# Where layer 2's weights, chunk 1's input blocks and tile 2's gathers stand in the start of a three-layer cross network

## The reference

```
inputs = emb[ids] * vals[:, :, None]            # 1024 x 39 x 16
h = inputs
for i in range(3):                              # 200 outputs each
    x = einsum('bhd,bmd->bhmd', h, inputs).reshape(B, -1, 16)
    x = relu(einsum('bcd,oc->bod', x, W[i]) + b[i][None, :, None])
    h, direct = (x[:, :100], x[:, 100:]) if i < 2 else (None, x)
    finals.append(direct)
cin = sum(concatenate(finals, 1), -1)
d = relu(relu(inputs.reshape(B, -1) @ D0.T + d0) @ D1.T + d1)
out = concatenate((cin, d), 1) @ fc_W.T + fc_b + sum(bias_emb[ids] * vals)
```

## Time and profile before

| | |
|---|---|
| median of 3 runs | 2751.63 us |
| profiled execution, its own time | 2752.34 us |
| its span | 2750.5 us |
| busy PE, DVE, ACT, POOL | 2649.5, 2285.0, 1834.6, 2249.6 us |
| chain that ended last, PE's share | 94% |
| PE idle before its first instruction | 62.6 us |

### The profile page before, as it was taken

How to read it: one execution, slowest core, us unless ns; L and a number is a source line. 1 busy time by engine, 2 the same in 40 slices (tenths; PEclk the granted TensorE clock), 3 DMA queues, 4 the chain that set the end, 5 groups by cost and what they waited for, 6 DMA issues and landing times.

```text
span 2750.5 us, 66670 instructions
## 1 busy us (share of the span) xinstructions
PE 2649.5 (96%) x17928; PEld 2640.2 (96%) x17928; DVE 2285.0 (83%) x4584; ACT 1834.6 (67%) x4776; POOL 2249.6 (82%) x1912
## 2 busy tenths in 40 slices
PE   0699999999999999999999999999999999999999
PEld 0599999999999999999999999999999999999998
DVE  2788888888888888888888888888888888888884
ACT  0576776766767667676777767677677766766663
POOL 6788888888888888888888888888888888877763
PEclk9799999999999999999999999999999999999999
DMA  8844545445444454544545455454554545545441
GB/s 149 199 124 123 133 126 130 124 118 144 116 133 125 118 149 112 136 121 122 146 111 138 120 131 137 114 136 118 138 131 118 133 117 140 129 117 136 111 115 51
DMA packets 199914, 349.82 MB, mean 127 GB/s; under 512 B 66632, under 2 KB 118697, under 8 KB 199615
## 3 DMA queue, kind: packets, MB, share of 16 engines
q1 hardware_dynamic: 185782, 342.81, 45.6%
q0 software_dynamic: 10496, 2.88, 3.1%
q10 hardware_dynamic: 3464, 2.68, 0.3%
HBM read 344.29 MB, written 14.17 MB: 130 GB/s over the span
## 4 chain that ended last, share of the span: by engine, by line
PE 94%; POOL 2%; SPq 2%; DVE 1%; issue 1%; DMA 1%; ACT 0%; POOLq 0%; ACTq 0%; DVEq 0%
PE acc L642 61%; PE acc L643 28%; PE acc L667 2%; POOL raw L498 1%; PE hrep L678 1%; DVE W L1061 0%; SPq L319 0%; DMA odd<-lin 0%; PE acc L742 0%; PE acc L743 0%; PE acc L744 0%; SPq L309 0%; DMA raw<-table,idx 0%; PE hrep L764 0%; PE hrep L766 0%
## 5 line engine op out<-in xcount | busy, mean ns | idle before, releaser
L642 PE MATMUL acc<-W,xhi_d 128*128 128x400 f32 x5632 | 1732.4, 367 | 17.2 <-DVE xlo_d L1087 10.6
L643 PE MATMUL acc<-W,xlo_d 128*128 128x200 f32 x5632 | 1434.9, 255 | 0.0
L1087 DVE TENSOR_TENSOR xlo_d<-prod_d,xhi_d 128x512 fp32r<-128x512 f32 (+1 forms) x1536 | 983.9, 641 | 205.1 <-ACT xhi_d L819 147.2
L1079 DVE TENSOR_TENSOR prod_d<-hrep,xrep 128x512 f32<-128x512 f32 (+1 forms) x1536 | 1039.0, 677 | 105.8 <-issue 27.7
L548 POOL TENSOR_TENSOR xlo_p<-prod_p,xhi_p 128x512 fp32r<-128x512 f32 (+1 forms) x768 | 953.8, 1242 | 181.3 <-ACT xhi_p L813 135.6
L642 PEld LDWEIGHTS acc<-W,xhi_d 128*128 128x128 f32 x5632 | 1059.9, 188 | 20.1 <-DVE xlo_d L1087 12.9
L643 PEld LDWEIGHTS acc<-W,xlo_d 128*128 128x128 f32 x5632 | 1078.4, 191 | 0.0
L819 ACT ACTIVATE xhi_d<-prod_d 128x512 fp32r<-128x512 f32 (+1 forms) x1536 | 885.1, 577 | 222.6 <-PE acc L643 199.8
L642 PE MATMUL acc<-W,xhi_p 128*128 128x400 f32 x2944 | 917.2, 363 | 12.9 <-POOL xlo_p L548 12.9
L542 POOL TENSOR_TENSOR prod_p<-hrep_s,xrep 128x512 f32<-128x512 f32 x512 | 665.9, 1301 | 161.3 <-ACT hrep_s L856 108.5
L643 PE MATMUL acc<-W,xlo_p 128*128 128x200 f32 x2944 | 751.7, 255 | 0.0
(11 more groups left out here) (92 smaller groups left out, 927.1 us busy)
## 6 DMA issues: line engine op xcount, KB each, us to landing
xrep<-xs SPq DMA_DIRECT2D x384, 384.0 KB
l0x<-xs SPq DMA_DIRECT2D x378, 136.5 KB
xrep<-xs SPq DMA_DIRECT2D x384, 128.0 KB
xrep<-xs SPq DMA_DIRECT2D x128, 336.0 KB
xrep<-xs SPq DMA_DIRECT2D x128, 64.0 KB
l0x<-xs SPq DMA_DIRECT2D x378, 19.5 KB
lin<-w SPq DMA_DIRECT2D x8, 750.0 KB
raw<-table,idx POOLq DMA_INDIRECT x328
```

Source lines behind the costliest of these rows:

```text
L642: pe.matmul(bank[:, 0:2 * OUTS], hi, w, start=first, stop=last, skip_group_check=True)
L643: return pe.matmul(bank[:, 0:OUTS], lo, w[:, 0:OUTS], start=False, stop=last, skip_group_check=True)
L1079: nc.vector.tensor_tensor(to, h, xrep[:, (par + layer - 1) % 2, a:a + count, :], ALU.mult).then_inc(s_prod_d, 1)
L1087: op = nc.vector.tensor_tensor(xlo_d[:, slot, 0:split], bank[:, 0:split], xhi_d[:, slot, 0:split].bitcast(F32), ALU.subtract)
```

## The change

Layer 2's rows are copied to DRAM by ACT's DMA queue, after layer 1's weights have landed and been rounded: three quarters ahead of ACT's first rounding of products, the last one behind it. ACT rounds all of layer 1's weights at that point. SP loads layer 2's weights before chunk 1's blocks. The five pieces of layer 2's weights are split in groups D0 to D4 of step 1 instead of D4 to D8, and the low part of piece 1 is made by POOL instead of DVE, in the middle of step 1. POOL gathers nothing in steps -1 and 0 and at the head of step 1: 4 rows at the end of step 1, 4 in each of steps 2 to 9 and 3 in step 10; its first pass through the loop is written out. For all tiles scaling, turning and storing come one step of the tile later.

```diff
-        W2_AT = {4: 0, 5: 1, 6: 2, 7: 3, 8: 4}
+        W2_AT = {0: 0, 1: 1, 2: 2, 3: 3, 4: 4}
-        def rows_of_weights(engine, layer, src):
+        def rows_of_weights(engine, layer, src, quarters):
...
@@ sync
-            rows_of_weights(sp, 2, w2)
-            sp.wait_ge(s_pt, 4)
             sp.wait_ge(s_prod_p, p_num(0, 1) + 1)
             load_layer0(2)
+            load_weights(sp, 2, w2)
+            sp.wait_ge(s_pt, 4)
             for e in (1, 2, 0, 3):
                 sp.wait_ge(s_xblk[e], BLOCK_SEM[e])
                 load_block(1, 1, e)
-            load_weights(sp, 2, w2)
...
-                    if j == 10:
+                    if j == 11:
                         store_inputs(k + 1)
-                    if j == 11:
+                    if j == 12:
                         store_dense_inputs(k + 1)
@@ gpsimd
-            FREE_AT = 8
+            FREE_AT = 9
             COUNTS = [2] * 5 + [3] * 9 + [2]
-            BEFORE = sum(COUNTS[0:DIM - 1 - FREE_AT])
+            FIRST = [4 * n + 4 for n in range(FREE_AT)] + [FIELDS]
...
+            product(1, 1, 2)
+            low(1, 1)
+            a, b = PIECES[2][1]
+            pool.wait_ge(s_whi, W_DONE[1] + 2)
+            nc.gpsimd.tensor_tensor(weights(2)[:, a:b, 1, :], raw_weights(2, a, b),
+                                    weights(2)[:, a:b, 0, :].bitcast(F32), ALU.subtract).then_inc(s_wlo2, 1)
+            product(1, 1, 3)
...
+            for m in range(FIRST[0]):
+                gather(m)
+            product(2, 0, 0)
+            low(1, 5)
...
+            for j in range(DIM):
+                tile_step(0, j, first_gathers)
+            with pool.Fori(1, TILES - 1) as k:
@@ scalar
             split_weights(0, 0)
+            for n in range(3):
+                split_weights(1, n)
+            rows_of_weights(act, 2, w2, range(3))
             high(-1, "P", 0)
             high(-1, "P", 1)
+            split_weights(1, 3)
+            split_weights(1, 4)
+            rows_of_weights(act, 2, w2, (3,))
             high(0, "P", 0)
@@ vector
-                    if isinstance(i, int) and i == 1 and d in W2_AT:
+                    if isinstance(i, int) and i == 1 and W2_AT.get(d, 1) != 1:
...
-                    if j == 9:
+                    if j == 10:
                         turn_inputs(k + 1)
```

More of the change, by code:

```diff
@@ L209, in rec_kernel @@
         s_wlo = sem("weights_low")
+        s_wlo2 = sem("second_piece_of_w2_low")
         s_ident = sem("ident_set")
@@ L289, in spread_of @@
             return (0, CHUNKS + 1) if isinstance(i, int) and i == CHUNKS else (layer - 1, i + 2 - layer)
[L291 to L294 removed]
+        W2_AT = {0: 0, 1: 1, 2: 2, 3: 3, 4: 4}
+        W_NEEDED = [{("P", 0): (s_wlo, 1)},
+                    {("D", 0): (s_wlo, 2), ("P", 2): (s_wlo, 3), ("D", 2): (s_wlo, 4), ("D", 4): (s_wlo, 5),
+                     ("D", 5): (s_wlo, 6)},
+                    {("D", 6): (s_wlo, 7), ("P", 4): (s_wlo2, 1), ("D", 8): (s_wlo, 8), ("D", 10): (s_wlo, 9),
+                     ("D", 11): (s_wlo, 10)}]
         def pairs(c):
@@ L299, in pairs @@
                 :, c * L0_SLOTS * L0_ROWS:(c + 1) * L0_SLOTS * L0_ROWS].rearrange("p (s r) -> p s r", r=L0_ROWS)
-        def rows_of_weights(engine, layer, src):
+        def rows_of_weights(engine, layer, src, quarters):
             used = H_QUARTER * FIELDS
             full = used // QUARTER
-            for q in range(4):
+            for q in quarters:
                 rows = lin[layer][used * q:used * (q + 1), :]
@@ L341, in _ @@
             sp.dma_start(val[:], vals.rearrange("(p t) m -> p (t m)", p=P)).then_inc(s_small, 16)
-            rows_of_weights(sp, 1, w1)
+            rows_of_weights(sp, 1, w1, range(4))
             sp.dma_start(fcw[:], fc_w.partition_broadcast(P)).then_inc(s_fc, 16)
@@ L552, in p_groups, with step @@
                 return [g for kind, g in step_order(i) if kind == "P"]
-            def step(i, par, ahead, rows=()):
+            def step(i, par, ahead):
                 mine = p_groups(i)
                 for at, k in enumerate(mine):
-                    for m in rows[at * len(rows) // len(mine):(at + 1) * len(rows) // len(mine)]:
-                        gather(m)
                     if at + 1 < len(mine):
@@ L585, in _ @@
             copy_idx(1, 1)
-            pool.wait_ge(s_xin, 3)
-            gather(0)
             product(-1, 1, 0)
@@ L595, in _ @@
             low(0, 1)
-            for m in range(1, 4):
-                gather(m)
             product(0, 0, 2)
@@ L600, in _, with tile_step, first_gathers @@
             low(0, 2)
-            for m in range(4, 7):
-                gather(m)
             product(1, 1, 0)
             low(0, 3)
-            for m in range(7, 9):
-                gather(m)
-            step(1, 1, 0, range(9, BEFORE))
-            with pool.Fori(0, TILES - 1) as k:
-                for j in range(DIM):
-                    gathers(j)
-                    if j == FREE_AT:
-                        scale(k + 1, True)
-                        copy_idx((k + 2) % TILES, k + 2)
-                    step(k * DIM + (j + 2), j % 2, 0)
+            pool.wait_ge(s_xin, 3)
+            product(1, 1, 1)
+            low(1, 0)
+            product(1, 1, 2)
[5 more added lines that the diff above has]
+            product(1, 1, 3)
+            low(1, 2)
+            product(1, 1, 4)
+            low(1, 3)
+            product(1, 1, 5)
+            low(1, 4)
+            for m in range(FIRST[0]):
+                gather(m)
+            product(2, 0, 0)
+            low(1, 5)
+            def tile_step(k, j, rows):
+                rows(j)
+                if j == FREE_AT:
+                    scale(k + 1, True)
+                    copy_idx((k + 2) % TILES, k + 2)
+                step(k * DIM + (j + 2), j % 2, 0)
+            def first_gathers(j):
+                if j < FREE_AT:
+                    for m in range(FIRST[j], FIRST[j + 1]):
+                        gather(m)
+                else:
+                    gathers(j)
+            for j in range(DIM):
+                tile_step(0, j, first_gathers)
+            with pool.Fori(1, TILES - 1) as k:
+                for j in range(DIM):
+                    tile_step(k, j, gathers)
             for i in range(2 + DIM * (TILES - 1), CHUNKS):
@@ L660, in multiply @@
                 if isinstance(i, int) and c == 0 and (kind, g) in W_NEEDED[layer]:
-                    pe.wait_ge(s_wlo, W_NEEDED[layer][(kind, g)])
+                    pe.wait_ge(*W_NEEDED[layer][(kind, g)])
                 for n, t in enumerate(tiles):
@@ L1050, in split_weights @@
                     a, b = PIECES[layer][n]
-                    done = W_DONE[layer] - len(PIECES[layer]) + n + 1
-                    dve.wait_ge(s_whi, done)
+                    dve.wait_ge(s_whi, W_DONE[layer] - len(PIECES[layer]) + n + 1)
                     src, hi, lo = raw_weights(layer, a, b), weights(layer)[:, a:b, 0, :], weights(layer)[:, a:b, 1, :]
@@ L1148, in _ @@
             first_layer0(1, (prod_d[2], acc[2]))
-            split_weights(1, [0, 1])
+            split_weights(1, [0])
             dve.wait_ge(s_fc, 32)
             evacuate(0, 0)
-            split_weights(1, [2])
+            split_weights(1, [1, 2])
             product(0, 0, 0)
             product(0, 0, 1)
+            split_weights(1, [3])
             product(0, 0, 2)
             low(0, 0)
-            split_weights(1, [3])
+            split_weights(1, [4])
             product(0, 0, 3)
             low(0, 1)
-            split_weights(1, [4])
             product(0, 0, 4)
```

10 lines of the change are left out of this document (1 added, 9 removed).

## The result

Changed kernel: 2758.26 us, the median of 22 runs (2755.16 to 2761.33); the kernel before on the same chip 2751.02 us (22 runs). The ratio is 1.0022, with a 95% interval of 1.0016 to 1.0029: slower by 6 us. The forecast was 2753.5 in a range of 2744.5 to 2763; the measured interval lies on both sides of the 0.2% that was to divide "same" from "slower". The profiled execution has a span of 2758.8 us, 8.3 more than before.

What follows compares the result with a forecast made beforehand. PE bounds the kernel from step 2 on, so step 2's start decides. POOL's work after block 0 at 113.4, 28.4 us plus 2, puts it at 143.8 against 142.65: +1.2 on 2752.34 gives 2753.5, range 2744.5 to 2763.

Steps and rivals of the forecast that it cites:

- PE's work from step 2 on is the same, so the time moves with the start of step 2: Steady part: PE is busy 2455.35 of 2457.35 us, so the change acts by moving step 2's start, now 142.65.
- locks: Step 1: DVE's weight splits and POOL exclude one another at SBUF, holding POOL 2 us, bounds 0 and 4.
- The copy: Start of the kernel: layer 2's copy on ACT's queue starts at 69.5, against 72.62, and ends at 88 (86 to 89).
- The same bytes go in the same time by either queue: Start of the kernel: with full DMA engines, two queues move 5 MB from 67 us no sooner, 4.7 MB by 85.
- ACT's delay of 7.4 us: Step 0: issuing the copy puts ACT's first rounding of a product at 76.8, not 69.38; hidden, so costed at nothing.
- The landings of chunk 1: Before step 1: layer 2 lands at 107, then block 1 at 109, 2 at 111, 0 at 113.4, 3 at 115.5.
- PE's rest of 4 us before it: Before step 1's first products: PE rests from about 107 to 111, waiting for chunk 1's blocks.
- POOL's row of work, 28.4 us and 2 of locks: Step 1: from block 0 at 113.4 POOL needs 28.4 us to step 2's first operand, plus 2 for DVE's splits.
- the 143.8: Start of step 2: PE begins it at 143.8 us, against 142.65 now, set by POOL.
- Four gathers a step at no cost: Steps 2 to 10: POOL's step takes 19.5 of PE's 20.2 us; cost nothing, up to 4 if stops fall there.
- Layer 2 really early: Faster rival, chance 0.20: two queues draw more, the load lands at 101, step 2 begins 6.8 us sooner; 2745.5.
- Chunk 1 starved: Slower rival, chance 0.30: the load lands at 112, block 0 at 118.4, past the deciding 116; +8.5 us, 2760.8.

Runs made afterwards that it cites:

- x7: The kernel before with only the copy of layer 2's weights on ACT's queue; ratio to before 0.9999.
- x2: The changed kernel with layer 1's first sum and its taking ahead of step 1's first products; ratio to before 1.0028.
- x1: The changed kernel with its first eight gathers moved to POOL's rest before product P2 of step 1; ratio to before 1.0007.
- x12: The changed kernel with the subtraction of layer 2's second piece back on DVE; ratio to before 1.0008.
- x6: The changed kernel with the splits of layer 2's weights back behind D4 to D8, POOL's subtraction behind P4; ratio to before 1.0040.
- x4: The kernel before with only the gathers' part of the change, scaling and turning one step later; ratio to before 0.9993.
- x8: x4 with the copy of layer 2's weights on ACT's queue as well; ratio to the kernel before 0.9986.
- x11: x8 with the subtraction of layer 2's second piece on POOL behind product P4; ratio to the kernel before 0.9995.
- x3: The changed kernel with chunk 1's input blocks again issued ahead of layer 2's load; ratio to the kernel before 1.0029.
- x9: x8 with SP issuing layer 2's load ahead of chunk 1's blocks; ratio to the kernel before 1.0010.
- x10: x8 with the splits of layer 2's weights behind D0 to D4 of step 1; ratio to the kernel before 1.0016.

## Why the prediction came out as it did, step by step

- **PE's work from step 2 on is the same, so the time moves with the start of step 2.** Right for the steps: from 622 us on the distance is constant over 2000 us. Not complete: the start moved by 2.89 us and cost 4.60, since after the 3.75 us rest PE ran about 4 us at the lower clock (0.57), and two more such stretches added 3.3 us of the span. The prediction put the clock at nothing and gave no reason. That 2758.3 lies in its range is in part luck: the range was made wide for landings, locks and gathers, and most of the miss of the span is the clock.
- **The copy.** Its start, 69.5 behind three roundings, was wrong: its DMAs were issued from 65.17 on beside the roundings. Its end, 88, was close: SP could issue the load at 86.00. "The same bytes go in the same time by either queue" was wrong for this stretch: in 67 to 85 us 5.6 MB were moved instead of 4.7, since both queues had work from the start. It held for the sum: alone, the copy on ACT moved layer 2 by 2.0 us (x7).

```profile
67.00:73.00 6.00, 0.00 (x0) 0.00 (x0) 5.38 (x6) 4.95 (x6) 3.52 (x3) 1.00 1.08 303
73.00:79.00 6.00, 4.15 (x14) 3.76 (x14) 0.74 (x4) 1.36 (x4) 5.17 (x6) 1.00 1.04 308
79.00:85.00 6.00, 2.37 (x15) 2.13 (x15) 6.00 (x5) 3.03 (x11) 3.90 (x3) 0.96 0.98 316
```

- **ACT's delay of 7.4 us.** The first rounding came at 70.22 and not near 77, 0.8 us late; the third came at 76.82, 3.1 us late. So the 7.4 us weren't there to be hidden, and no run puts their cost at nothing to the test.
- **The landings of chunk 1.** Block 1 at 109 (DVE at 109.94) and block 0 at 113.4 (POOL at 112.81): right within a us. Layer 2's own landing at 107 can't be read, since its first rounding stands behind D0's (111.17).
- **PE's rest of 4 us before it.** This is a step that failed. It rested 13.90 us. PE was through with the steps before at 102.96 and not at 107, and the prediction ended the rest with the landing of block 1 and overlooked that PE's D0 needs layer 1's bank, whose summing stood behind products D0 to D2 and the first split on DVE. x2 shows that this cost nothing by itself here, since POOL came later.
- **POOL's row of work, 28.4 us and 2 of locks.** The mechanism was right (x1, x2, x12), the size was off: 32.6 us from 112.81 to 145.4. Subtraction of the weights 3.61 (3.9 forecast). The term that was mis-sized is the locks: 2.58 for a subtraction that takes 1.0, then 2.88, 2.04, 1.43 and 1.91 where 1.25 stood, together 4.8 us instead of 2, and outside the bounds of 0 to 4. The other terms were 0.6 us smaller and the landing 0.6 earlier, which leaves the 1.7 us by which step 2 came after the 143.8.
- **Four gathers a step at no cost.** Right in steps 2 to 10: no distance grows there. The stop of 6.48 us, for which the prediction kept "up to 4", moved with the 114th gather to the next step, and PE ran at the lower clock behind it, 1.7 us. That is no price of the gathers. The lower clock (0.59 to 0.66 in the 4 us behind PE's rest) stands there in four traces, of the change, x6, x2 and x12, and the distance grows by 1.7, 1.8, 1.1 and 1.3 us. In the other ten, x1, x4 and x8 to x11 with the same gathers among them, the clock is 1.00 and the distance moves by 0.6 us or less, up or down.
- **The end.** 2.0 us more in the last 90 us, 1.6 of them at the lower clock behind the last fixed point (0.83). x1 has the same program there, a clock of 1.00 and 0.2 us; x7, with the gathers of the kernel before, has the 0.83. So the change doesn't make it, and why one execution has it and another doesn't stays open.
- **The rivals.** *Layer 2 really early* got the 2 us of x7, not its 6.8. Its rate was right (303 to 316 GB/s, against its 319) and its end of the copy nearly (86.00, against 84); what failed is that the load and the blocks behind it went no faster for that: block 0 was there at 112.81 and not at 107.4. *Chunk 1 starved* (2760.8) had the right sign and place; block 0 landed before its point of 116, and what took its part is the locks and the clock.
- **Two slips in its working.** Its bound for a load as slow as layer 1's is 88 + 25 = 113 and not 112. And the first of the two waits that it read on DVE, 3.5 us from 88.78, ran over three POOL instructions and not two (rows below).

What the sum couldn't show: it compared the changed kernel with the one before as a whole and found +1.2, and never asked for each part alone. In the spans the parts were -3.3 us (gathers), -1.0 to -3.2 (copy) and +4 to +9 for each of the three others, and the small sum hid them.

## What to carry to other kernels

When a fill waits for two transfers, the one whose consumers can work without the other goes first, and nothing that needs the other is queued in front of them, on any engine. An engine that is given a long piece of work "because it is idle" is idle only until the landing that releases everything; count its row of work from there. And undo parts from both ends: two edits that make the same wait look free when undone singly (x3, x6), and each costs 8 to 9 us when added singly (x9, x10). Last, look at the clock of both traces before a difference of 2 us between two spans is given a cause: here three stretches at the lower clock made 5.0 of 8.3 us, and two of them came and went from one trace to the next.
